# A vision transformer layer on one core: forty transposes and twenty-two products that nobody reads, added to TensorE's order

## The reference, cut to what matters

```python
# x: (32, 3, 96, 96) images -> 32 x 36 patches of 768 numbers = 1152 rows = 9 tiles of 128
p = img2patches(x, 16, 16)
h = layernorm(p, ln1_g, ln1_b) @ W + b            # 768 -> 192
h = layernorm(h, ln2_g, ln2_b)
# attention, 12 heads of 16, over the batch index (32 keys per query), q and k normalised
qkv = layernorm(h) @ in_proj_weight.T + in_proj_bias
attn = softmax((q/|q|) @ (k/|k|).T * exp(min(logit_scale, LOGIT_SCALE_MAX)))
h = h + ((attn @ v) * head_scale) @ out_w.T + out_b
# feed forward, 192 -> 2*512 -> 192, inputs quantised to 8 bits per row, weights to -1, 0, 1
up, gate = split(bitlinear(layernorm(h), w_in, g_in))
h = h + bitlinear(silu(gate) * up, w_out, g_out)
```

## Time and profile before

| | us |
|---|---|
| median of 3 runs | 140.63 |
| the runs | 140.28, 140.63, 143.15 |
| the profiled execution | 140.62 |
| its span, first to last instruction | 138.7 |
| TensorE, VectorE, ScalarE, GpSimd busy | 105.4, 108.2, 81.6, 66.0 |
| mean granted TensorE clock | 0.918 |

### The profile page before, as it was taken

One profiled execution on the slowest core, in us unless ns is written; L12 is line 12 of the kernel. 1 busy time (PEld: TensorE's weight loads), 2 busy tenths in 40 slices (PEclk: granted clock), 3 DMA queues, 4 the chain that ended last, 5 costly groups with the idle time before them and its releaser, 6 DMA issues.

```text
span 138.7 us, 4589 instructions
## 1 busy us (share of the span) xinstructions
PE 105.4 (76%) x1784; PEld 82.0 (59%) x1784; DVE 108.2 (78%) x388; ACT 81.6 (59%) x168; POOL 66.0 (48%) x160
## 2 busy tenths in 40 slices
PE   0003999999989999999997954989799877655610
PEld 0003999888778798986866642657676644234400
DVE  4059028999999999999999998959999999695210
ACT  0305246998987669523836582065589789786400
POOL 7003001565329621486136866614874798787000
PEclk9999999999999999999999997579999997797555
DMA  4999999996000000000000000000000010000110
GB/s 99 225 243 263 176 171 264 156 175 132 2 0 0 5 2 5 5 2 5 5 0 5 0 5 0 5 2 5 5 5 10 23 33 28 21 26 13 42 44 29
DMA packets 24093, 7.75 MB, mean 56 GB/s; under 512 B 20038, under 2 KB 23495, under 8 KB 24072
## 3 DMA queue, kind: packets, MB, share of 16 engines
q1 hardware_dynamic: 20310, 6.43, 24.4%
q10 hardware_dynamic: 3762, 1.03, 3.9%
HBM read 6.58 MB, written 0.88 MB: 54 GB/s over the span
## 4 chain that ended last, share of the span: by engine, by line
PE 30%; DVE 30%; ACT 13%; POOL 9%; issue 8%; DMA 4%; ACTq 2%; DVEq 0%
PE bank L612 5%; PE bank L594 4%; PE bank L613 4%; DMA xs<-in_x_dram 4%; PE bank L624 4%; POOL yw L337 3%; PE bank L585 3%; PE bank L529 2%; DVE pT L878 2%; DVE bst L764 2%; DVE mx L869 2%; ACTq L232 2%; PE bank L686 2%; ACT xp L441 2%; DVE ax L933 1%
## 5 line engine op out<-in xcount | busy, mean ns | idle before, releaser
L594 PE MATMUL bank<-w_emb_g,xT 128*128 128x192 f32 x108 | 19.6, 331 | 0.0
L585 PE MATMUL bank<-ident,xp 128*128 128x128 f32 x54 | 8.2, 292 | 12.6 <-ACT xp L441 12.6
L594 PEld LDWEIGHTS bank<-w_emb_g,xT 128*128 128x128 f32 x108 | 17.4, 190 | 0.6 <-ACT xT L448 0.2
L612 PE MATMUL bank<-w_qkv,xhT 97*128 97x384 f32 (+1 forms) x36 | 13.4, 455 | 2.2 <-DVE on L886 1.8
L299 POOL TENSOR_TENSOR rs<-mv,mhalf 128x1 f32<-128x1 f32 x9 | 5.3, 589 | 19.6 <-DVE mv L786 19.6
L585 PEld LDWEIGHTS bank<-ident,xp 128*128 128x128 f32 x54 | 6.6, 150 | 13.1 <-issue 12.6
L764 DVE BATCH_NORM_STATS2 bst<-xs 128x6 f32<-128x384 f32 x18 | 8.8, 538 | 6.1 <-DMA xs<-in_x_dram 6.1
L337 POOL TENSOR_TENSOR yw<-yy,gout_bc 128x512 f32<-128x512 f32 x9 | 11.4, 1267 | 4.0 <-DVE yy L929 3.8
L613 PE MATMUL bank<-w_qkv,xhT 96*128 96x384 f32 (+1 forms) x36 | 12.7, 437 | 0.0
L669 PE MATMUL bank<-wi_t,xqT 96*128 96x512 bf16 x36 | 10.2, 409 | 1.4 <-ACT xqT L488 1.2
L441 ACT ACTIVATE xp<-xs,mv 128x768 f32<-128x768 f32 x9 | 8.3, 929 | 4.8 <-DVE mv L770 4.6
(11 more groups left out here) (135 smaller groups left out, 304.4 us busy)
## 6 DMA issues: line engine op xcount, KB each, us to landing
xs<-in_x_dram SPq DMA_DIRECT2D x30, 96.0 KB, 3.6
out_dram<-h_all SPq DMA_DIRECT2D x18, 48.0 KB
wi_raw<-in_L_ffn_w_in_dram SPq DMA_DIRECT2D x1, 768.0 KB, 7.3
xs<-in_x_dram ACTq DMA_DIRECT2D x6, 96.0 KB, 4.0
w_emb_sb<-in_L_tok_W_dram SPq DMA_DIRECT2D x1, 576.0 KB, 7.0
w_qkv_raw<-attn_in_proj_weight_dram ACTq DMA_DIRECT2D x1, 432.0 KB
wo_raw<-in_L_ffn_w_out_dram SPq DMA_DIRECT2D x1, 384.0 KB, 8.5
gout_bc<-in_L_ffn_g_out_dram SPq DMA_DIRECT2D x1, 256.0 KB, 4.0
```

What stands on the lines that cost most here:

```text
L585: mm = nc.tensor.transpose(dst, xp[:, t % 3, P * k:P * (k + 1)], ident[:, :])
L594: mm = nc.tensor.matmul(emb_bank, xT[:, t % 3, P * k:P * (k + 1)], w_emb_g[:, 3 * (k % 2) + k // 2, :], start=(k == 0), stop=(k == KF - 1))
L612: nc.tensor.matmul(dst, xhT[:, t % 3, 0, :], w_qkv[:, 0, cols], start=True, stop=False)
```

## The change

`warm(n)` is called eight times ahead of everything else on TensorE; each call transposes the identity five times into the same 128 columns of bank 0. `keep(n, dst)` multiplies a 96 x 128 piece of the bf16 identity by 512 columns of the first feed-forward weight, n times, into a bank that is free then. It is called at seven places: four products before `qkv(8)`, three before `xqT_(7)`, three before `xqT_(8)`, four before `yqT_(6)`, two before `yqT_(7)`, two before `ff2(6)` and four before `yqT_(8)`. Nothing reads what they write. No other engine's program and no other order is changed.

```diff
+            def warm(n):
+                if n == 0:
+                    pe.wait_ge(c_id, 1)
+                for _ in range(5):
+                    nc.tensor.transpose(xT_lo[:, 0:P], ident[:, :], ident[:, :])
+
+            def keep(n, dst, *freed):
+
+                pe.wait_ge(c_idb, 1)
+                pe.wait_ge(p_wiE, 2)
+                wait_all(pe, freed)
+                for _ in range(n):
+                    nc.tensor.matmul(dst[:, :], ident_b[0:HC, :], wi_t[:, 0, 0:FF], start=True, stop=True)
+
...
+            for n in range(8):
+                warm(n)
             xT_(0); bmm(); xT_(1, (xT_ok, 2)); emb(0, (p_bias, 1)); qkvT(); xT_(2, (xT_ok, 4)); emb(1, (h0s_ok, 1))
...
-            xhT_(8); qkv(8, (qk_ok, 8), (on_ok, 5)); sc(6, (h2_ok, 4)); oT_(4); xqT_(3, (oT_ok, 5)); pv(5, (vx_ok, 9))
+            xhT_(8); keep(4, xT_lo, (xT_ok, 2 * T)); qkv(8, (qk_ok, 8), (on_ok, 5)); sc(6, (h2_ok, 4)); oT_(4); xqT_(3, (oT_ok, 5)); pv(5, (vx_ok, 9))
...
-            proj(8, (h2_ok, 8)); yqT_(3); xqT_(6); ff1(6, (yg_ok, 6), (yy_ok, 6)); ff2(3, (out_ok, 3)); xqT_(7); yqT_(4)
-            ff1(7, (yg_ok, 7), (yy_ok, 7)); ff2(4, (out_ok, 4)); xqT_(8); ff1(8, (yg_ok, 8), (yy_ok, 8)); yqT_(5)
-            yqT_(6, (yqT_ok, 6)); ff2(5, (out_ok, 5)); yqT_(7, (yqT_ok, 7)); ff2(6, (out_ok, 6)); ff2(7, (out_ok, 7))
+            proj(8, (h2_ok, 8)); yqT_(3); xqT_(6); ff1(6, (yg_ok, 6), (yy_ok, 6)); ff2(3, (out_ok, 3)); keep(3, bank[6], (h2_ok, T)); xqT_(7); yqT_(4)
+            ff1(7, (yg_ok, 7), (yy_ok, 7)); ff2(4, (out_ok, 4)); keep(3, bank[6], (h2_ok, T)); xqT_(8); ff1(8, (yg_ok, 8), (yy_ok, 8)); yqT_(5); keep(4, bank[6], (h2_ok, T))
+            yqT_(6, (yqT_ok, 6)); ff2(5, (out_ok, 5)); keep(2, bank[6], (h2_ok, T)); yqT_(7, (yqT_ok, 7)); keep(2, bank[6], (h2_ok, T)); ff2(6, (out_ok, 6)); ff2(7, (out_ok, 7)); keep(4, bank[6], (h2_ok, T))
             yqT_(8); ff2(8, (out_ok, 8))
```

## The result

The changed kernel takes 145.51 us (median of 4, 144.9 to 147.38), the kernel before beside it 140.45. The ratio is 1.037, 95% interval 1.028 to 1.045: slower, where a small gain was forecast. The profiled execution took 145.18, its span 143.1 against 138.7.

What follows compares the result with a forecast made beforehand. VectorE was taken as the busy engine from 20 to 85 us, with low-clock TensorE stretches making it wait and queued stores at the end. Gains of 1.55 + 0.6 + 0.1 = 2.25 us off 140.62 gave 138.4, range 136.4 to 141.4.

Steps and rivals of the forecast that it cites:

- The forty transposes in themselves: At TensorE's start: they end near 10.3 us, at the least near 6.3, in idle time before 12.65, and cost nothing.
- the value of the early clock: At `xT_(0)` and `bmm`: clock low again, value 0; the rival that it stays up gave 137.4 us, chance 0.15.
- the term of 1.55: Middle, at `qkv(8)`: `keep(4)` holds the clock, VectorE starts `mx(6)` 1.55 us earlier, and this carries on.
- The two `keep(3)`: Near 117 us, at `ff1(7)`: with the clock held, `yw(7)` and tile 5's `out_` come 0.6 us earlier.
- the store queue: At the end: stores of tiles 5 to 8 take 9.5 us in a queue, whatever tile 8 does, ending 0.6 earlier.
- tile 8: At the end: the last tile would be finished near 131.1 instead of 132.87, 1.8 us earlier.
- The term of 0.1 beyond tile 5: At the final stores: 0.1 us gained beyond the 0.6, between ends of 0 and 1.2.
- The unexplained stall goes: Rival, in `pv(4)`: added instructions shift TensorE's program, VectorE gets back a 0.7 us wait; 137.7 us, chance 0.12.
- Slower: the shift makes a second such stall: Rival, in a burst of small products: another 1.65 us stall and a clock fall, 141.6 us; slower cases together 0.12.
- The sum of 1.55, 0.6 and 0.1: Middle, near 117 and the end together: 2.25 us off 140.62, forecast 138.4 us.
- The other direction of the same rival: In `pv(4)`: the stall falls where TensorE waits anyway, VectorE gains 0.7 us at 83; 137.7 us, chance 0.12.

Runs made afterwards that it cites:

- e4: The changed kernel plus 88 transposes of 32 x 32 behind the forty, 256 instructions ahead in all; ratio 0.986 to the kernel before, median 139.7 us.
- e12: The kernel before with all keep calls and no forty transposes, one execution for its trace; 139.07 us, span 137.2.
- e15: The kernel before with 88 small transposes at the start and 16 before `qkv(2)`, no keep; span 137.4 us against 138.7.
- e13: The kernel before with all keep calls, 88 small transposes at the start and 16 before `qkv(2)`; span 135.4 us against 138.7.
- e3: The kernel before with forty transposes of 32 x 32 at the start and no keep; ratio 1.055, 148.0 us.
- e16: The kernel before with all keep calls and no forty transposes, a repeat; no separate time given, keep only is quoted at 0.979 to 0.987.
- e9: The changed kernel with 104 transposes of 32 x 32 in place of the forty, all keep calls; 141.3 us.
- e2: The changed kernel without any keep call, the forty transposes left in; ratio 1.063 to the kernel before, median 150.4 us.
- e6: The changed kernel with 32 transposes of 32 x 32 in place of the forty, all keep calls; time not given, within the expected 141 to 146 us.
- e1: The changed kernel without the forty transposes, all keep calls left in; ratio 0.987 to the kernel before, median 140.35 us beside 140.99.
- e14: The changed kernel with 88 transposes of 32 x 32 in place of the forty, all keep calls; ratio faster, median slower, traced execution 142.3 us.

## Why the prediction was wrong, point by point

- **The forty transposes in themselves: right.** They start at 1.51, last 7.1 us (bounds 4.7 to 8.7) and end at 8.6, before the first real work. The clock falls only at 13.5, later than forecast: `xT_(0)` still ran at the full level (0.84 instead of 1.51), but `bmm` waited for VectorE's `b_wide` and then took 3.74 at the low level until 16.9, so the value of the early clock is 0. e4 and keep only agree within their intervals (0.986 and 0.979 to 0.987), which shows it without the shift. That the transposes don't wait for one another was right as well.
- **The rule of the Trainium skill ("TensorE: Matmul & The Clock Gate", Part 4), that transposes don't raise the clock: the trace disagrees.** In the changed kernel the granted clock's record turns to full at 6.7 us, when nothing but transposes of 128 x 128 had run since 1.51. Twenty-five of them start in the 5.2 us before that, one each 0.22, and the last fifteen one each 0.11. The rows call them fp32 products and don't tell whether the mode that the page means was on.
- **`keep(4)`: the mechanism right, the term of 1.55 about right, where the clock was held.** The gain of VectorE over the stretch is 1.7 in e12 (1.43 seen at `mx(6)`), 1.8 between e15 and e13, and 1.7 between e3 and the changed kernel. That the clock is held was too much to count on: it fell in five of twelve traces with `keep`. And that the 1.55 carries on held in e13 and the changed kernel alone: in e12, e16, e4 and e9 the clock falls once more near 93, behind an idle stretch of TensorE before `xqT_(3)` (1.28 us in e12), and in e12 VectorE loses 0.6 of its gain there.
- **The two `keep(3)`: right.** `yw(7)` has no wait before it in the changed kernel, nor in e12, where VectorE's `yy(7)` set it before. Measured against the kernel before, VectorE gains 0.6 between 113 and tile 5's `out_` in both, which is the term.
- **The end: the store queue right, tile 8 mis-sized.** From the end of tile 5's `out_` to the end of the span it is 11.7 us before (138.7 - 127.02), 11.7 in the changed kernel (143.1 - 131.38) and 11.6 in e12. The four tiles' stores again take 9.5 us at 41 GB/s. The term of 0.1 beyond tile 5 is 0. Tile 8 was finished 5.8 us behind tile 5 before and 5.3 now (136.31 - 130.97), 0.5 nearer and not 1.2; the stores hide the error.
- **The step that failed: "The unexplained stall goes" and "Slower: the shift makes a second such stall".** I had seen the stall of 1.65 us and that the added instructions would shift the program against its cause. The sum of 1.55, 0.6 and 0.1 has no term for that shift. It was put at nothing, and as a rival it was one stall more, with a chance of 0.12 together with another mechanism and a time outside the range. The runs put in its place: a block end every 256 instructions, at which TensorE can stall where a burst of small instructions runs up to it within some 2.7 us of the start of its fetch. With 80 instructions ahead five of them do, 5.9 us against 1.65 before and 1.1 in keep only. The four long ones put VectorE back by 5.2 us. The low clock from 78.4 to 85.2 adds 2.7; it begins at or up to 2.1 us behind the end of the stall at 1985 in all four traces that have that stall (the changed kernel, e2, e3, e6), and no other trace is at the low level there. It was not tried by itself.
- **The other direction of the same rival was right.** With the stall gone, e15's VectorE gains 0.8 us at 83, and 0.7 was forecast.
- **The cause could have been seen beforehand, the number could not.** The page before shows q8 with 14 fetches and 0.23 MB, the trace a fetch at 80.68 and the stall that ends at 83.36. Counting instructions up to it would have given 2241; with the changed program's 80 more, the points lie 80 instructions earlier in the old work, in other bursts. How many of them stall can't be told from that.

Open: what makes a fetch start when it does. In the two traces of before and after it starts from 0.4 us before to 6.3 us after the previous block's end is passed, and this decides which of the points stall. So the number of stalls can't be told for a new shift; 176, 192 and 208 were found by trying. Theory D rests on the traces with the late load against all others, and on e13 and e15, where the fetch was moved and the load was on time; how one fetch of 16 KB holds up a load by over 1 us isn't shown. Nor is it shown why the same `keep(4)` holds the clock in one execution and not in another.

## What to carry to other kernels

Before adding instructions to an engine that runs bursts of small ones, look for idle time without a releaser in the middle of a burst and for an instruction fetch 2 to 3 us before its end; if there is one, the number of instructions ahead is a parameter of the kernel, to be tried at several values over one block of 256. A comparison of two kernels that differ in the number of instructions ahead of such bursts compares their alignment too: a control with the same work and a shift of a whole block (e4) takes it out. Products that nobody reads can hold the clock and be worth 1 to 2 per cent where the engine waits for others (e13 against e15), but not in every execution, and only if their count doesn't move the blocks into the bursts. Look at the median of all executions beside the best ones before you count on such a gain: in e1 it was half a per cent, in e14 it was none.

## What the runs showed of the hardware that was not expected

- TensorE's instructions come by fetches of 16 KB, 256 instructions; a stall ends 2.15 to 2.72 us after the start of its fetch, in 28 of 28 cases at recorded instruction 256 k + 193. With `keep` in all of them, the shift alone moved the ratio to the kernel before between 0.98 and 1.04.
- Forty transposes of 32 x 32 that last 2.3 us in idle time at the start cost 5.5 per cent, by stalls that begin 60 us later (e3).
- With the first 16 KB fetch at 9.3 to 10.4 us, amid a load of 576 KB, the load took 8.3 to 8.5 us to land instead of 6.9 to 7.2, and VectorE was 1.5 us later behind it (e9 against e13).
- Behind the same four products and the same idle time of 1.97 us the granted clock stayed at 1.00 in e9 and fell to 0.50 in e14.
- Transposes of 128 x 128 alone brought the clock to full, at 6.7 us, having begun at 1.51.
